# A sequential convolution sweep on TensorE: each tap in four column tiles of 32 outputs instead of two of 64

## The chip, the cores and the metric

One core of one Trainium2 chip runs the whole program. The metric is device time in microseconds (us) of one execution, the median of several. TensorE (PE) multiplies, ScalarE (ACT) and VectorE (DVE) read PSUM and do the elementwise work, GpSimd (POOL) helps a little, and SyncE (SP) issues most DMAs.

## What is computed

The reference is a two-layer network on an image of shape (8, 32, 64, 64): layer norm over channels, a spectral convolution, an expert block on tokens, again a layer norm, then four directional sweeps, and a second expert block. The change touches only the sweeps:

```python
def _sweep(x, w, b, axis, reverse):          # w is (32, 32, 9), b is (32,)
    rows = jnp.moveaxis(x, axis, 0)
    if reverse:
        rows = rows[::-1]
    def step(prev, row):
        new = row + jax.nn.relu(_conv1d(prev, w, b))   # 9 taps along the row, 32 -> 32 channels
        return (new, new)
    _, rest = jax.lax.scan(step, rows[0], rows[1:])
    ...
out = _sweep(x, w_d, b_d, axis=2, reverse=False)
out = _sweep(out, w_u, b_u, axis=2, reverse=True)
out = _sweep(out, w_r, b_r, axis=3, reverse=False)
out = _sweep(out, w_l, b_l, axis=3, reverse=True)
```

Each sweep is a chain of 63 steps, and a step needs the whole result of the step before it. Four sweeps make 252 steps.

## The kernel before

Everything stays in SBUF; all matmuls that matter here are float32. The program is written out by hand for each engine, with semaphores between them, and the order of the text is the order of each engine's queue.

**A step.** A row of 64 positions is folded on the partitions: 4 position groups of 32 channels make 128 partitions, and the 16 positions of a group lie in the free dimension, with one zero column at each end (`state`, four slots). The 9 taps and the folding become three banded 128 x 128 matrices per sweep (`conv_sb[:, s, d]`, d = 0, 1, 2), so that a step is three matmul taps that accumulate in PSUM. The batch of 8 is cut into two halves h of 4 images (64 moving columns each), and each has its own PSUM bank (`conv_bank`), so that one half can be multiplied while the other is being finished.

**Who does what in a step.** PE (lines 673 to 683) waits for a half's state (`s_st`), then issues for each tap d two matmuls, o = 0 and 1, each for 64 of the 128 output rows. The moving operand is the same for both; the weights are a 64-column slice, and the output goes to PSUM partitions 0 to 63 or 64 to 127. This is column tiling: the two matmuls stand in two halves of the array. The last matmul of a half raises `s_cv`. DVE (lines 1085 to 1092) then computes max(conv, -bias) + row + bias in one instruction per half and raises `s_st`, which releases PE for the next step of that half. ACT (lines 809 to 850) adds the bias to the row that comes two steps later (`fetch`, line 811) and copies the new state into the image (`archive`, line 815, `s_arc`).

In the profile every float32 matmul call stands as two weight loads (PEld) and two matmul records (PE): 252 steps x 2 halves x 3 taps x 2 tiles = 3024 calls, 6048 records. The two pairs of a call go to the same column tile and follow each other directly, before the pairs of the next call.

**Loops.** Each sweep does its first three steps straight, then 15 passes of a loop of four steps (`pe.Fori(1, HO)`), on every engine.

**Around the sweeps.** After the second sweep the image is re-folded from rows to columns, after the fourth back again. Both are done by many small DMAs, cut into pieces that are issued while the sweep that writes the data still runs: `move_rows` (line 294; pieces of 5, 5, 4 and 2 groups, 16 DMAs each) and `move_columns` (line 305; three pieces of 16 DMAs, then two half pieces). Each piece waits for `s_arc`. SP issues them; of the last piece POOL issues 6 of 16. On POOL these stand behind `add_conv` (line 317), which adds the finished columns. The third sweep starts when the first columns are there (`wait_columns`, line 288), and the second expert block needs the last columns through `add_conv` on DVE (line 319, called from line 999).

Of the kernel before, what the change touches and what calls it, by code (L numbers as in the profile page):

```python
# [8 lines left out]
B, C, H, W = 8, 32, 64, 64  # L9
# [5 lines left out]
Q = 4  # L15
# [6 lines left out]
HB, MO = B // 2, P // 2  # L22
# [15 lines left out]
def build_kernel(nc, x_in, dft, wspec, conv_w, conv_b, gate_w, gate_b, w1, w2, b2, own, out):  # L38
# [5 lines left out]
    with ExitStack() as ctx:  # L44
        def sb(name, shape, dt=F32):
            return ctx.enter_context(nc.sbuf_tensor(name, shape, dt))
# [14 lines left out]
        conv_sb = sb("conv_sb", [P, 4, 3, P])  # L61
# [61 lines left out]
        def blk(region, n):  # L123

            return region[:, n * P:(n + 1) * P]

        def banks(b0, nb):
            return PS[:, b0:b0 + nb, :].rearrange("p k c -> p (k c)")
# [129 lines left out]
        def half_count(s, t, h):  # L258

            return 2 * row_count(s, t) - 1 + h  # L260

        def state_slot(s, u):

            return (u + 3 * (s % 2)) % 4

        def conv_bank(u, h):

            return PS[:, 2 * h + u % 2, 0:HB * HO].rearrange("p (b v) -> p b v", b=HB)
# [115 lines left out]
        def _(pe):  # L384
# [60 lines left out]
            for l in range(2):  # L445
                m = pe.matmul(PS[:, 6 + l, 0:BL * NE], centre, gate_sb[:, l, :], start=True, stop=True)
# [50 lines left out]
            for c in range(NCH):  # L497
# [5 lines left out]
                for w, full, read in ((1, s_t1, s_tmp), (0, s_t0, s_comb)):  # L503
                    if c >= 2:
                        pe.wait_ge(read, c - 1)
                    for x in range(X8):
                        m = pe.transpose(blk(banks(4 * (c % 2) + 2 * w, 2), x), Z[:, c, x, w], ident)  # L507
# [165 lines left out]
            for s in range(4):  # L673
                def step(q, u):
                    for h in range(2):
                        pe.wait_ge(s_st, half_count(s, Q * q + u - 1, h))
                        for d in range(3):
                            prev = state[:, state_slot(s, u - 1), HB * h:HB * (h + 1), d:d + HO]
                            for o in range(2):
                                m = pe.matmul(conv_bank(u, h)[MO * o:MO * (o + 1)],  # L680
                                              conv_sb[:, s, d, MO * o:MO * (o + 1)], prev,
                                              start=(d == 0), stop=(d == 2))
                        m.then_inc(s_cv, 1)

                for u in range(1, Q):
                    step(0, u)
                with pe.Fori(1, HO) as q:
                    for u in range(Q):
                        step(q, u)
# [480 lines left out]
```

## Time and profile before

| | |
|---|---|
| Median of 3 executions | 669.88 us (669.1 to 671.66) |
| The profiled execution, own time | 670.63 us |
| its span, first to last instruction | 668.8 us |
| mean granted TensorE clock | 0.944 of 2.4 GHz |
| PE / PEld / DVE / ACT / POOL busy | 596.1 / 533.3 / 392.3 / 358.2 / 43.2 us |
| sweeps, from the first matmul to the last DVE result | 308.7 to 564.4 us |
| of that, the re-folding between sweeps 2 and 3 | 431.6 to 442.3 us |

The busy time of PE is that of overlapping records (a record lasts about four times the distance between two), so it says little on how full the array is. The distances between starts and the idle time before an instruction say more. "x24" counts records. The granted clock is 1.00 (2.4 GHz) or 0.50 (1.2 GHz) at any moment; in between are means of a stretch.

### The profile page before, as it was taken

Reading aid. Unit: us, or ns where it says so; the run is one execution under the profiler, and the core shown is the slowest. Engines: PE = TensorE matmul, PEld = TensorE weight load, DVE = VectorE, ACT = ScalarE, POOL = GpSimd, SP = SyncE. Lnnn points to the kernel's source line nnn. Section 1 sums busy time; section 2 is a strip of 40 time slices with the busy share of each in tenths; the row PEclk is TensorE's granted clock in tenths of the full one; section 3 lists DMA queues with packets and bytes.
Section 4 is the critical chain, followed back from the end, with each engine's and each line's share of the span. In section 5 each row is a group of like instructions: output and inputs, shape, how many; then the busy total and the mean of one; then the engine's idle time right before and its main releaser. Section 6 shows DMA issues by size and latency. Waiting matters only on the chain.

```text
span 668.8 us, 23180 instructions
## 1 busy us (share of the span) xinstructions
PE 596.1 (89%) x9536; PEld 533.3 (80%) x9536; DVE 392.3 (59%) x888; ACT 358.2 (54%) x844; POOL 43.2 (6%) x30
## 2 busy tenths in 40 slices
PE   8977886999997999997999999769999999677897
PEld 8877776999996986896888888658888888676883
DVE  3748988555469615554555555425555554498216
ACT  4767987452278101344666666437776665478200
POOL 4000000000030000000000000100000244310000
PEclk9999988999997989996999999969999999897889
DMA  9631771060000000000000032320000334200006
GB/s 360 267 126 30 262 277 68 1 252 1 2 0 1 2 17 0 1 1 1 0 0 0 1 73 61 80 39 0 0 0 2 63 67 79 44 0 1 1 2 251
DMA packets 54386, 40.70 MB, mean 61 GB/s; under 512 B 49350, under 2 KB 49478, under 8 KB 53126
## 3 DMA queue, kind: packets, MB, share of 16 engines
q1 hardware_dynamic: 53816, 39.29, 18.4%
q8 instruction: 33, 0.54, 0.3%
q0 software_dynamic: 384, 0.39, 0.3%
q10 hardware_dynamic: 144, 0.39, 0.2%
q14 instruction: 9, 0.07, 0.0%
HBM read 27.49 MB, written 4.19 MB: 47 GB/s over the span
## 4 chain that ended last, share of the span: by engine, by line
PE 67%; DVE 17%; SPq 6%; ACT 5%; issue 3%; DMA 1%; POOL 0%; ACTq 0%; DVEq 0%
PE PS L680 31%; PE PS L408 6%; DVE RB L940 5%; PE PS L654 5%; PE PS L607 5%; SPq L313 4%; PE PS L429 3%; DVE sums L980 2%; PE PS L483 2%; DVE RCD L992 2%; PE PS L558 2%; PE PS L507 2%; PE PS L514 2%; SPq L302 2%; PE PS L528 2%
## 5 line engine op out<-in xcount | busy, mean ns | idle before, releaser
L680 PE MATMUL PS<-RE,conv_sb 128*64 128x64 f32 x6048 | 238.2, 229 | 18.8 <-DVE RE L1083 8.5
L680 PEld LDWEIGHTS PS<-RE,conv_sb 128*64 128x64 f32 x6048 | 204.8, 140 | 52.5 <-DVE RE L1090 36.6
L1090 DVE SCALAR_TENSOR_TENSOR RE<-PS,negb_sb,RE 128x64 f32<-128x64 f32 x504 | 143.0, 284 | 106.2 <-PE PS L680 80.6
L811 ACT ACTIVATE RE<-RCD,convb_sb 128x128 f32 (+1 forms) x126 | 50.5, 402 | 47.5 <-DVE RE L1090 47.5
L747 ACT COPY RB<-PS 32x128 f32<-32x128 f32 x128 | 47.7, 373 | 8.2 <-PE PS L467 6.8
L940 DVE COPY RB<-PS 32x128 f32<-32x128 f32 x128 | 48.2, 376 | 6.0 <-PE PS L467 4.4
L483 PE MATMUL PS<-RE,RB 128*64 128x64 f32 x1024 | 35.0, 233 | 14.5 <-DVE RCD L949 7.8
L483 PEld LDWEIGHTS PS<-RE,RB 128*64 128x64 f32 x1024 | 33.8, 148 | 16.1 <-DVE RB L940 11.5
L811 ACT ACTIVATE RE<-RE,convb_sb 128x128 f32 (+1 forms) x63 | 32.3, 513 | 20.8 <-DVE RE L1090 15.6
L429 PE MATMUL PS<-warm 128*128 128x128 bf16 x468 | 37.2, 250 | 6.6 <-ACT RCD L787 4.0
L429 PEld LDWEIGHTS PS<-warm 128*128 128x128 bf16 x468 | 34.5, 114 | 7.7 <-ACT RCD L787 4.4
L866 DVE TENSOR_REDUCE sums<-RE 128x32 f32<-128x1024 f32 x16 | 19.4, 1218 | 34.2 <-ACT RE L719 34.2
L811 ACT ACTIVATE RE<-RB,convb_sb 128x128 f32 (+1 forms) x63 | 25.3, 402 | 22.6 <-DVE RE L1090 22.6
L815 ACT COPY RCD<-RE 128x128 f32 (+1 forms) x126 | 35.5, 282 | 1.6 <-DVE RE L1090 1.6
L815 ACT COPY RB<-RE 128x128 f32 (+1 forms) x126 | 35.6, 282 | 1.5 <-DVE RE L1090 1.5
L719 ACT ACTIVATE RE<-PS 128x1024 f32<-128x1024 f32 x16 | 16.2, 1021 | 33.7 <-PE PS L408 33.7
L654 PE MATMUL PS<-RCD,espread 128*128 128x512 f32 x64 | 31.6, 650 | 0.0
L408 PEld LDWEIGHTS PS<-dft_sb,RCD 128*128 128x128 f32 x128 | 30.5, 328 | 0.9 <-issue 0.5
L408 PE MATMUL PS<-dft_sb,RCD 128*128 128x128 f32 x128 | 30.8, 396 | 0.0
L708 ACT COPY RCD<-PS 128x256 f32<-128x256 f32 (+1 forms) x40 | 24.7, 692 | 11.1 <-PE PS L665 6.0
L766 ACT COPY RB<-PS 128x512 f32<-128x512 f32 (+1 forms) x24 | 16.2, 736 | 26.2 <-PE PS L514 26.2
L588 PE MATMUL PS<-proj,RA 128*128 128x192 f32 x128 | 23.8, 348 | 6.1 <-ACT RB L780 5.7
(115 smaller groups left out, 781.2 us busy)
## 6 DMA issues: line engine op xcount, KB each, us to landing
RE<-wspec SPq DMA_DIRECT2D x8, 2048.0 KB, 8.3
RA<-x_in SPq DMA_DIRECT2D x8, 512.0 KB, 7.7
RCD<-x_in SPq DMA_DIRECT2D x1, 4096.0 KB, 13.2
out<-RA SPq DMA_DIRECT2D x8, 512.0 KB, 2.7
RCD<-RB SPq DMA_DIRECT2D x48, 64.0 KB, 2.1
RE<-RCD SPq DMA_DIRECT2D x32, 80.0 KB, 2.2
RE<-RCD SPq DMA_DIRECT2D x16, 64.0 KB, 2.1
RCD<-RB SPq DMA_DIRECT2D x26, 32.0 KB, 1.9
```

The source lines that it names most:

```text
L313: eng.dma_start(CO[C * bl:C * bl + C, k, i, w0:w0 + Q * (v1 - v0)], XF[C * i:C * i + C, Q * v0:Q * v1, BH * bl:BH * bl + BH, :]).then_inc( ...
L408: m = pe.matmul(blk(ln_slot(g), n), src, centre, start=True, stop=True)
L429: pe.matmul(PS[:, bank, 0:P], warm[:, :], warm[:, :], start=True, stop=True)
L483: m = pe.matmul(o[:, x % 2, y], XB[:, c % 2, x, 2 * y + a].rearrange("p r q b -> p (r q b)"), WR[:, c % 3, a, x, y, :], start=True, stop=True)
L607: m = pe.matmul(PS[:, 4 + bh, 0:P], blk(centred(l, 2 * (t // 8) + bh), t % 8), WTOK[:, t, :], start=(t == 0), stop=(t == NT - 1))
L654: pe.matmul(PS[:, 4 + k % 4, :], espread[:, BL * bh:BL * bh + BL, :].rearrange("p b o -> p (b o)"), rhs, start=True, stop=True).then_inc(s ...
L680: m = pe.matmul(conv_bank(u, h)[MO * o:MO * (o + 1)], conv_sb[:, s, d, MO * o:MO * (o + 1)], prev, start=(d == 0), stop=(d == 2))
L747: m = act.copy(o, i)
L811: act.activation(rowb[:, u], row_at(SRC[s], s, q, u), ACT.Identity, bias=convb_sb[:, s:s + 1]).then_inc(s_row, 1)
L815: act.copy(row_at(DST[s], s, q, u), state[:, state_slot(s, u), :, 1:1 + HO]).then_inc(s_arc, 1)
L940: m = dve.tensor_copy(o, i)
L1090: dve.scalar_tensor_tensor(out=state[:, state_slot(s, u), k, 1:1 + HO], in0=conv_bank(u, h), scalar=negb_sb[:, s:s + 1], in1=rowb[:, u, k] ...
```

## The change

One loop of the step is widened: four matmul calls per tap instead of two, each with 32 weight columns and 32 PSUM partitions (`C` is 32, `MO` is 64, `Q` is 4). What is added up is the same, the waits and increments are the same, and the last call of a half still raises `s_cv`.

```diff
                         for d in range(3):
                             prev = state[:, state_slot(s, u - 1), HB * h:HB * (h + 1), d:d + HO]
-                            for o in range(2):
-                                m = pe.matmul(conv_bank(u, h)[MO * o:MO * (o + 1)],
-                                              conv_sb[:, s, d, MO * o:MO * (o + 1)], prev,
+                            for o in range(Q):
+                                m = pe.matmul(conv_bank(u, h)[C * o:C * (o + 1)],
+                                              conv_sb[:, s, d, C * o:C * (o + 1)], prev,
                                               start=(d == 0), stop=(d == 2))
                         m.then_inc(s_cv, 1)
```

PE gets 6048 calls in the sweeps instead of 3024. The other engines' programs do not change.

## Rows read from the trace of the kernel before

**Rows 1.** The page: TensorE in 40 slices, clock, and two groups of its part 5.
```profile
PE   8977886999997999997999999769999999677897
...
PEclk9999988999997989996999999969999999897889
...
L680 PE MATMUL PS<-RE,conv_sb 128*64 128x64 f32 x6048 | 238.2, 229 | 18.8 <-DVE RE L1083 8.5
L680 PEld LDWEIGHTS PS<-RE,conv_sb 128*64 128x64 f32 x6048 | 204.8, 140 | 52.5 <-DVE RE L1090 36.6
L1090 DVE SCALAR_TENSOR_TENSOR RE<-PS,negb_sb,RE 128x64 f32<-128x64 f32 x504 | 143.0, 284 | 106.2 <-PE PS L680 80.6
```
**Rows 2.** Windows, line 680 alone: stretch, its us, busy (records) of PE, of PEld, clock, DMA share, GB/s.
```profile
317.28:431.10 113.82, 109.32 (x2856) 93.04 (x2856) 1.00 0.11 28
...
308.72:314.63 5.91, 5.91 (x106) 5.90 (x108) 0.50 0.00 0
...
442.66:447.75 5.09, 5.08 (x92) 5.08 (x94) 0.50 0.09 14
```
**Rows 3.** Timeline of weight loads and DVE in one step at full clock: start, us, what.
```profile
320.15 0.78 PEld L680 LDWEIGHTS PS<-RE,conv_sb 128*64 128x64 f32 x24 [0.17 <-DVE RE L1090]
...
320.16 0.28 DVE L1090 SCALAR_TENSOR_TENSOR RE<-PS,negb_sb,RE 128x64 f32<-128x64 f32 x1
320.77 0.28 DVE L1090 SCALAR_TENSOR_TENSOR RE<-PS,negb_sb,RE 128x64 f32<-128x64 f32 x1 [0.32 <-PE PS L680]
```
**Rows 4.** Chain of waits and timeline: runs of matmuls elsewhere (start, us, what).
```profile
74.67 3.72 PE PS L483 x120
...
176.44 3.59 PE PS L558 x32
```
**Rows 5.** Windows, line 637 alone (32 weight columns, 8 moving columns).
```profile
245.92:246.33 0.41, 0.41 (x13) 0.41 (x14) 1.00 0.00 0
```
**Rows 6.** Line 680 in windows (full, then half clock) and whole: duration ns least/median/most.
```profile
L680 PEld LDWEIGHTS PS<-RE,conv_sb x4: 133/134/136, 320.1 to 320.2; 128*64 128x64 f32 x4
L680 PE MATMUL PS<-RE,conv_sb x2: 270/270/270, 320.1 to 320.2; 128*64 128x64 f32 x2
...
L680 PE MATMUL PS<-RE,conv_sb x4: 316/342/369, 310.1 to 310.2; 128*64 128x64 f32 x4
...
L680 PE MATMUL PS<-RE,conv_sb x6048: 221/221/369, 308.7 to 563.9; 128*64 128x64 f32 x196
```
**Rows 7.** Windows, line 680, first half step of sweep 3, half clock: records under way.
```profile
442.66:442.70 0.04, 0.03 (x2) 0.03 (x2) 0.50 0.52 74
442.70:442.72 0.02, 0.02 (x2) 0.02 (x2) 0.50 0.26 39
442.72:442.74 0.02, 0.02 (x2) 0.02 (x4) 0.50 0.11 13
442.74:442.82 0.08, 0.08 (x2) 0.08 (x4) 0.50 0.02 2
442.82:442.84 0.02, 0.02 (x4) 0.02 (x5) 0.50 0.00 0
442.84:442.90 0.06, 0.06 (x4) 0.06 (x6) 0.50 0.00 0
442.90:442.94 0.04, 0.04 (x5) 0.04 (x4) 0.50 0.00 0
```
**Rows 8.** Timeline of DVE: the step after the first loop pass, and both ends.
```profile
316.87 0.70 DVE L1090 SCALAR_TENSOR_TENSOR RE<-PS,negb_sb,RE 128x64 f32<-128x64 f32 x2 [0.26 <-PE PS L680]
317.90 0.63 DVE L1090 SCALAR_TENSOR_TENSOR RE<-PS,negb_sb,RE 128x64 f32<-128x64 f32 x2 [0.33 <-PE PS L680]
...
430.98 0.63 DVE L1090 SCALAR_TENSOR_TENSOR RE<-PS,negb_sb,RE 128x64 f32<-128x64 f32 x2 [0.32 <-PE PS L680]
...
563.78 0.64 DVE L1090 SCALAR_TENSOR_TENSOR RE<-PS,negb_sb,RE 128x64 f32<-128x64 f32 x2 [0.32 <-PE PS L680]
...
578.94 1.92 DVE L319 TENSOR_TENSOR RA<-RCD 128x1024 f32<-128x1024 f32 x1 [8.80 <-DMA RCD<-RB]
```
**Rows 9.** Timeline of the issuing queues, SP and POOL, at both re-foldings.
```profile
424.71 10.42 SPq L302 DMA_DIRECT2D RE<-RCD  x16
...
432.25 3.62 POOL L302 DMA_DIRECT2D RE<-RCD  x6 [230.61 <-ACT RCD L815]
...
560.58 16.98 SPq L313 DMA_DIRECT2D RCD<-RB  x26
...
562.06 5.69 POOL L319 TENSOR_TENSOR RA<-RCD 128x1024 f32<-128x1024 f32 x2 [9.51 <-DMA RCD<-RB]
```
**Rows 10.** The page, part 3: the queue that carries TensorE's instructions.
```profile
q8 instruction: 33, 0.54, 0.3%
```

## The prediction

> **What bounds the kernel now.** I read the page first. TensorE is busy in nearly every slice, and the costliest groups are the sweeps' matmuls and weight loads and the DVE instruction that answers them [rows 1]. Busy says little here, since a record lasts four to eight times the distance to the next. So I read the windows: at full clock 2856 records, that is 119 steps of 24, take 113.82 us, or 0.956 us a step [rows 2]. Then one step in the timeline: the 24 weight loads cover 0.78 us, and before them PEld was idle for 0.17 us and waited for DVE [rows 3]. So the step is a latency chain and not yet a full array. For one half it is: PE's 12 records, the drain, 0.28 us of DVE, the way back.
>
> The change alters only PE's part, so I need to know when a matmul really starts.
>
> *How long an array slot is.* Line 558 streams 128 columns with 128-column weights: 32 records in 3.59 us, 0.112 each, so 0.056 for 64 columns [rows 4]. Line 483 has the shape and the two tiles of line 680: 120 records in 3.72 us, less the 0.22 of the last record [rows 6], are 0.0294 each, two in 0.0588 [rows 4]. So two column tiles each do one record in about the time one record needs alone: they do overlap. I call 0.0585 us a slot, with 0.056 as the lower bound. Before, a half is six slots.
>
> *What starts when.* The first half step of sweep 3 comes after a long pause, at half clock, with both tiles empty [rows 7]. At 442.66 to .70 the first call's two loads and two matmuls are on record (two each). By 442.74 the second call's loads have begun too (four loads). But up to 442.82 there are still only two matmuls; the third starts at about 442.83. How long does a 64-column load take? The first matmuls show it: 270 ns where the normal one is 221 at full clock, and 369 where it is 316 at half clock (most and least of the window of four) [rows 6], so some 0.05 us at either clock. The second tile's weights, started by 442.74, are there by 442.79, and its part of the array is empty. Its matmul still waits until about 442.83. That is just when the first call's first record has streamed (from 442.72, for the 0.107 us of a slot at half clock) and its second record can begin. My reading: matmuls start in program order, across tiles. A record that waits for its own tile holds up those behind it, whichever tile they are for.
>
> **The change, part by part.**
>
> *1. Matmuls.* With this rule, number the records of a tap: T0a T0b T1a T1b T2a T2b T3a T3b. Each b is for the same tile as its a and starts one slot later. T1a starts with T0b, T1b a slot later with T2a, and so on: every slot starts two records, as before. Two tiles overlap, never four. A tap has 8 records, so four slots; a half has 12 slots instead of 6, a step 24. At 0.0585 that is 1.404 us.
>
> Is that the bound, or still the chain? The chain of a half was 0.956 us, and gets six slots longer (0.351) and a shorter first load. Loads of 32 columns come 13 to 14 in 0.41 us [rows 5], 0.031 each instead of the 0.05 above, so 0.02 off. The chain is then 1.29 us, below 1.404. So PE's idle 0.17 us goes, PE becomes the bound, and DVE and ACT get slack. The extra 1 to 2 hundredths of shorter loading are hidden in a full array.
>
> Sweeps 1 and 2 run from 308.72 to 431.61 (430.98 + 0.63), 122.9 us [rows 2, 8]. After: the first 5.9 us are at half clock [rows 2], where a slot is 0.107 and a step 2.57, so 2.3 steps; the other 123.7 take 173.7; drain and the last DVE 0.5. Sum 180.1, +57.2. Sweeps 3 and 4, 442.66 to 564.42: 121.8 us. After: 5.1 at half clock (2.0 steps), 124.0 x 1.404 = 174.1, 0.5: 179.7, +57.9. I assume the clock comes back after as long a time; TensorE is at least as busy as before. Together **+115.1 us**. With 0.056 as the slot it would be 15 less, with 0.0588 2 more.
>
> *2. The loop's branch.* The step after the first pass comes 1.03 us after its predecessor instead of 0.956 [rows 8]: going back costs 0.07 more than the 0.17 us of idle time hides. In later passes it is hidden. That cover is now gone. Each of the 60 passes may cost from nothing (if enough instructions are queued ahead) to 0.24 us, 0 to 14 in all. Twice the instructions also means that a queue of a given depth covers less. I take 0.08, **+5 us**; the sum of the sweeps is so much larger that I do not refine it.
>
> *3. DMA pieces.* SP needs 10.42 us for 16 issues [rows 9]. The last two pieces of `move_rows` are 8 steps apart, 7.65 us now. So SP, which began at 424.71, is free only at 435.1, while POOL, with the same wait, began at 432.25. With 8 steps of 1.40 = 11.2 us SP is free in time: **-3 us**, as the columns' landing starts sweep 3. At the other end SP issues 26 DMAs from 560.58 without a pause to 577.56 [rows 9], though the last state was there at 564.4: it was late already at 560.58. After, only the last 10 issues (6.5 us) and 1.9 for landing follow the last step: 9 instead of 14.5 us until DVE's line 319 at 578.94 [rows 8]. POOL's adds also end before the last step instead of at 567.75. DVE had been idle for 8.80 us before line 319; POOL's and ACT's squares of the next stage start to show, so of 5.5 I take **-4.5**. Bounds together -9 to 0.
>
> Nothing else moves: ACT, DVE and POOL have the same instructions. The sum is 115.1 + 5 - 7.5 = +112.6 us. On the profiled execution's 670.63 that is 783.2; the median lies 0.75 below, so **782.5 us**. The bounds above (-15 to +2, -5 to +9, -1.5 to +7.5) add up to 761 to 801; they will hardly all fall to one side, so 764 to 798.
>
> **The rivals.**
>
> *Four tiles at once (faster).* If each tile had its own queue, T1a, T2a, T3a would start a few hundredths apart, a half would stay at six slots, the first load would be 0.02 to 0.027 shorter, and the last tile would start about 0.02 after the first instead of 0.0585. The chain would lose 0.06 us: 252 x 0.06 = 15, so 655 us. For it: two tiles do overlap fully [rows 4]. Against it: the empty second tile that waits in [rows 7]. It decides whether T1a starts before T0b. The Trainium skill has this as its rule: "TensorEngine Tiling (Array Packing)", When to Use Tiling, gives four column tiles for 32 columns, and "TensorE: Matmul & The Clock Gate", Part 3, has matmuls in different tiles start about 4 ns apart. The same Part 3 says that matmuls start and end strictly in order, which [rows 7] agree with; its bursts have one matmul per tile and not a pair that must follow each other. Chance 0.08.
>
> *Only the loads are in order (a little slower).* If matmuls were free but weight loads dispatched in order, the next tile would be held by one load of 0.031 per record pair. A tap is then 4 x 0.031 = 0.126 instead of 0.117, the end of a half 0.03 later, 252 x 0.03 = +8: 678 us. The second tile's matmul in [rows 7] waits 0.04 longer than its load would explain. Chance 0.05.
>
> *Worse than two at a time.* Either 32-column tiles do not overlap at all (48 slots, 2.8 us a step, about 1125 us), or the longer loop body does not stay in TensorE's instruction store. The body of four steps grows from about 196 to 388 instructions (four times 24 or 48 pairs of load and matmul, and a few of the loop). Queue 8 moved 0.54 MB in 33 packets in the whole program [rows 10], so the 60 passes now run without a refetch, but no row shows how much fits. A fetch of a microsecond or two in 30 to 60 passes would be 50 to 100 us on top, 830 to 880. The Trainium skill, "Runtime: NRT & Kernel Launch", Instruction fetch mechanics, speaks both of a store on TensorE that would hold the body and of a window of two pages that a branch must stay in; no run here has shown either. Chance 0.05.
>
> *No effect.* The widened loop is unconditional and lies on every step, so only an exact cancelling would give it: 0.02.
>
> **How the numbers follow.** Forecast 0.80, with its own range 764 to 798. That range leaves out the others, 0.20, so it is the range given. What this kernel's measurement can tell from no change is about 0.5%, 3.4 us. Faster by more: 0.08. Within: 0.02. Slower: 0.80 + 0.05 + 0.05 = 0.90.
>
> **What would show it.** In the profile after: 12096 records of line 680 in each of PE and PEld; at full clock a step of 1.39 to 1.42 us; no or little idle time of PE inside the sweeps; DVE's wait per half longer. In windows of the first half step of sweep 3, the matmuls still start two per slot, at 0.107. The PE side of line 1090's waits grows. SP begins the last piece of `move_rows` within a microsecond of POOL. If instead the step is near 0.90 us, matmuls do not wait across tiles, and my reading of [rows 7] is wrong; if it is 0.98, loads pace them. If steps are 1.40 but four-step passes are far above 5.7, the branch or the fetch costs more than I took. If PE shows a slot other than 0.0585 for 32 columns, the size of the term is off, not its sign.

## The result, and the profile after

| | before | after |
|---|---|---|
| median of 20 executions each, us | 670.16 (667.05 to 672.52) | 674.71 (670.94 to 678.59) |
| ratio | | 1.0069, 95% interval 1.0049 to 1.0089 |
| profiled execution, own time / span, us | 670.63 / 668.8 | 673.60 / 671.8 |
| mean granted clock | 0.944 | 0.947 |
| step at full clock, us | 0.956 | 0.950 |

The kernel became slower by 4.6 us, 0.7%. The forecast was +112.6 us. The sign was right by luck, for a reason that turned out to be false. The profiled executions differ by 3.0 us; only these can be taken apart below, and what the medians differ by beyond that no trace shows.

The page after, in the parts that answer to [rows 1] and [rows 10]:

```profile
span 671.8 us, 35276 instructions
...
PE   8977877999997999988999899669999999577897
...
PEclk9999989999997989996999999959999999897889
...
q8 instruction: 38, 0.62, 0.4%
...
L680 PE MATMUL PS<-RE,conv_sb 128*32 128x64 f32 x12096 | 228.8, 225 | 30.3 <-DVE RE L1083 8.5
...
L680 PEld LDWEIGHTS PS<-RE,conv_sb 128*32 128x32 f32 x12096 | 188.6, 111 | 70.8 <-DVE RE L1090 58.4
...
L1090 DVE SCALAR_TENSOR_TENSOR RE<-PS,negb_sb,RE 128x64 f32<-128x64 f32 x504 | 142.8, 284 | 108.4 <-PE PS L680 86.2
```

The number of records has doubled, 6048 to 12096, and yet PE is busy for less time and sits idle *more*: before the weight loads 70.8 us instead of 52.5, and still waiting for DVE. PE has not become the bound. The instruction queue moved 38 packets instead of 33.

Windows of line 680 after (stretch, its us, busy and records of PE, of PEld, clock, DMA share, GB/s), and one step in the timeline, which answer to [rows 2, 3]:

```profile
392.00:430.00 38.00, 35.67 (x1920) 29.43 (x1920) 1.00 0.31 78
```
```profile
330.08 0.72 PEld L680 LDWEIGHTS PS<-RE,conv_sb 128*32 128x32 f32 x48 [0.23 <-DVE RE L1090]
...
330.08 0.28 DVE L1090 SCALAR_TENSOR_TENSOR RE<-PS,negb_sb,RE 128x64 f32<-128x64 f32 x1
330.69 0.28 DVE L1090 SCALAR_TENSOR_TENSOR RE<-PS,negb_sb,RE 128x64 f32<-128x64 f32 x1 [0.33 <-PE PS L680]
```

1920 records are 40 steps of 48, in 38.00 us: 0.950 us a step. 48 loads now take 0.72 us where 24 took 0.78, and the idle time grew from 0.17 to 0.23. The latency chain is what it was.

**Four matmuls at once.** The same stretch as [rows 7], at half clock. (That stretch is called the first half step of sweep 3; it belongs to the second step. The first step, 24 records, had run at 438.09 before, and runs at 438.94 after.)

```profile
441.81:441.85 0.04, 0.03 (x4) 0.03 (x5) 0.50 0.48 68
...
441.89:441.96 0.07, 0.07 (x8) 0.07 (x12) 0.50 0.03 4
...
441.98:442.04 0.06, 0.06 (x9) 0.06 (x9) 0.50 0.00 0
```

Four matmul records are under way where two were, and eight about a slot later. [Rows 7] had two, then four. Each slot has simply doubled its content. With the forecast's rule (T0b holds back T1b and all behind it) this could not be.

**Where the 3.0 us of the profiled executions went.** Line 680's first record comes 0.44 us earlier and DVE's last result 1.64 us later, so the sweeps with the re-folding take 2.1 us longer. The steady steps gave back 252 x 0.0065 = 1.6. Against that stand four things, each read as the lengthening of DVE's steps against the steady one.

*First, TensorE stopped for code.* Weight loads in the first pass of sweep 2's loop, in the timeline:

```profile
373.06 0.26 PEld L680 LDWEIGHTS PS<-RE,conv_sb 128*32 128x32 f32 x15 [0.30 <-DVE RE L1090]
373.93 0.12 PEld L680 LDWEIGHTS PS<-RE,conv_sb 128*32 128x32 f32 x4 [0.61 <-issue]
...
375.99 0.33 PEld L680 LDWEIGHTS PS<-RE,conv_sb 128*32 128x32 f32 x15
377.37 0.14 PEld L680 LDWEIGHTS PS<-RE,conv_sb 128*32 128x32 f32 x2 [1.05 <-issue]
```

"issue" says that the engine waited for nothing that the profile shows. The middle of a half, after 15 loads, has no semaphore to wait for. From load to load the two stops are 0.72 and 1.16 us instead of about 0.01 to 0.05; a third of 0.42 us stands at 510.16, in sweep 4's first pass. The first two lie exactly 256 TensorE instructions apart. Together the three are 2.3 us, and they lengthen the steps by 1.9, since some idle time would have been there anyway. In the whole trace before there is no such stop inside the sweeps. The fetch packets on the instruction queue start about 1.2 us after TensorE enters each such block of 256, and the block behind can be used 2.2 us after that here, and up to 2.75 us in the runs below: 3.4 to 4.0 us for a block of new code. Two tiles use up 256 instructions in 5.1 us, four in 2.5 to 2.7. These stops stand in first passes of a loop, where the code is new.

*Second, the slow clock lasted longer.* TensorE has little or nothing to do between sweeps 2 and 3. Windows before, then after (all engines; the clock is the third number from the end):

```profile
434.00:438.00 4.00, 0.00 (x0) 0.00 (x0) 0.18 (x2) 0.18 (x1) 1.87 (x4) 0.51 0.61 118
...
447.00:452.00 5.00, 5.00 (x123) 4.45 (x121) 2.88 (x11) 3.40 (x10) 0.00 (x0) 0.92 0.01 3
```
```profile
434.00:438.00 4.00, 0.00 (x0) 0.00 (x0) 0.00 (x0) 0.00 (x0) 2.68 (x5) 0.87 0.69 140
...
447.00:452.00 5.00, 4.79 (x194) 4.46 (x190) 2.27 (x8) 2.42 (x8) 0.00 (x0) 0.64 0.02 3
```

The clock fell at 434.1 before and at 437.0 after, in the middle of a pause that ended nearly alike, and it came back at 447.8 and at 450.6. Much of the difference passed in waiting for the columns' DMAs: from sweep 3's first record to DVE's third step it is 6.98 us before and 7.02 after. Of the four steps behind that, two ran at half clock before and all or most of four after (1.28 us and not 0.95); they take 4.50 us before and 4.99 after. So the slow clock cost about 0.5 us.

*Third*, the step that follows the first pass of a loop is 1.23 us instead of 0.96 in sweep 2 and 1.39 instead of 1.03 in sweep 3; in sweeps 1 and 4 the two kernels are within 0.02 of each other. Together that is 0.7 us.

*Fourth*, the later passes are not free. Their first steps are now and then longer, most of all in sweep 3's fifth pass, beside one more fetch packet at 463.43:

```profile
462.80 0.62 DVE L1090 SCALAR_TENSOR_TENSOR RE<-PS,negb_sb,RE 128x64 f32<-128x64 f32 x2 [0.33 <-PE PS L680]
463.90 0.62 DVE L1090 SCALAR_TENSOR_TENSOR RE<-PS,negb_sb,RE 128x64 f32<-128x64 f32 x2 [0.47 <-PE PS L680]
```

That step is 1.09 us; the others are up to 1.05. All later passes together cost 0.5 us more than in the trace before. -1.6 + 1.9 + 0.5 + 0.7 + 0.5 is 2.0, against the measured 2.1.

The rest, 1.4 us, is lost behind the sweeps, between DVE's last result and its line 319 (14.52 us before, 15.92 after). The end in the timeline, as in [rows 8, 9]:

```profile
559.56 21.03 SPq L313 DMA_DIRECT2D RCD<-RB  x30
...
565.41 0.64 DVE L1090 SCALAR_TENSOR_TENSOR RE<-PS,negb_sb,RE 128x64 f32<-128x64 f32 x2 [0.31 <-PE PS L680]
...
581.97 1.92 DVE L319 TENSOR_TENSOR RA<-RCD 128x1024 f32<-128x1024 f32 x1 [10.19 <-DMA RCD<-RB]
```

SP's issues cost 0.65 us each before (16.98 for 26), 30 of them 19.6; here they took 21.03, since a single one, at 574.07, took 1.95. DVE's line 319 begins 3.03 us later than in [rows 8], and the span is 3.0 us longer.

The long issue is bound up with TensorE's code too. A fetch packet on TensorE's instruction queue runs from 574.16 to 575.60. In the 13 traces of this document 15 issues of the re-foldings are longer than 1 us (1.08 to 1.95), and every one overlaps such a packet. Of the re-foldings' DMAs 37 took over 2.6 us from issue to landing (the median is 2.07), and 36 of them were under way during one. The trace before has its long issue as well, 1.63 us at 439.51 beside a packet at 439.36, but in the first re-folding. Where a packet falls into the last issues, the pause before line 319 is 15.6 to 16.3 us in the kernels with a step of 0.90 to 0.96 us; in the two without one there (before and e7) it is 14.5. The one trace of before has no packet in this stretch; the changed kernel, e9, which is the same kernel again, and e11, which has its four tiles in reverse, all have one. What is shown is the coincidence, in every trace; no run moves the fetch alone. (Packet times are those of the traces' DMA records.)

### The profile page after: what moved, and what is told of

Same layout as the page of the kernel before. It is cut to its first block, busy times and chain, and to the rows that moved or that the text cites. A ratio compares the mean times of both kernels' runs of the same rounds, so it can differ in the third digit from the quotient of the medians.

```text
span 671.8 us, 35276 instructions
## 1 busy us (share of the span) xinstructions
PE 585.3 (87%) x15584; PEld 515.7 (77%) x15584; DVE 392.2 (58%) x888; ACT 358.4 (53%) x844; POOL 43.4 (6%) x30
## 4 chain that ended last, share of the span: by engine, by line
PE 57%; DVE 25%; SPq 6%; ACT 5%; issue 5%; DMA 1%; POOL 0%; ACTq 0%; DVEq 0%
PE PS L680 21%; DVE RE L1090 9%; PE PS L408 6%; DVE RB L940 5%; PE PS L654 5%; PE PS L607 5%; SPq L313 4%; PE PS L429 3%; DVE sums L980 2%; SPq L302 2%; DVE RCD L992 2%; PE PS L558 2%; PE PS L483 2%; PE PS L507 2%; PE PS L514 2%
## 5 line engine op out<-in xcount | busy, mean ns | idle before, releaser
L680 PE MATMUL PS<-RE,conv_sb 128*32 128x64 f32 x12096 | 228.8, 225 | 30.3 <-DVE RE L1083 8.5
L680 PEld LDWEIGHTS PS<-RE,conv_sb 128*32 128x32 f32 x12096 | 188.6, 111 | 70.8 <-DVE RE L1090 58.4
L483 PE MATMUL PS<-RE,RB 128*64 128x64 f32 x1024 | 34.1, 230 | 15.6 <-DVE RCD L949 8.1
```

What stands on the lines that cost most here:

```text
L483: m = pe.matmul(o[:, x % 2, y], XB[:, c % 2, x, 2 * y + a].rearrange("p r q b -> p (r q b)"), WR[:, c % 3, a, x, y, :], start=True, stop=True)
L680: m = pe.matmul(conv_bank(u, h)[C * o:C * (o + 1)], conv_sb[:, s, d, C * o:C * (o + 1)], prev, start=(d == 0), stop=(d == 2))
```

## The experiments

The question after the result was not whether four tiles overlap, but which rule gives 0.950 us, and why the kernel is nevertheless slower. I took four groups of runs: the order of the calls, the number and the width of tiles, where the code stands, and no tiles at all. Totals of single runs scatter by some 0.4%, so in the first two groups I compare the step at full clock, read from the distances of DVE's records.

### Order of the calls

**e1_tile_major_64.** Two tiles of 64, but all taps of tile 0 before those of tile 1.

```diff
-for d in range(3):
-    for o in range(2):
+for o in range(2):
+    for d in range(3):
```

> Two tiles of 64 as before, but the three taps of tile 0 are issued first and then the three of tile 1 (o outside, d inside). Theory A (each tile takes its records as they come, calls to another tile pass a call that waits, as far as TensorE looks ahead): if it looks ahead six records or more, the step stays at 0.956 us at full clock; if only to the next call, the tiles run one after the other, some 11 to 12 slots of 0.0585 a half, 1.29 to 1.40 us a step. Theory B (the strict order of the prediction, with two records a slot only because neighbouring calls are for different tiles): 11 slots a half, 1.3 to 1.4 us a step, total 755 to 785 us.

Measured: 705.1 us (before beside it: 673.38), and a step of 1.113 us, between the two expectations. Windows of line 680 in one half, which was released at 340.155:

```profile
340.16:340.26 0.10, 0.10 (x1) 0.10 (x2) 1.00 0.00 0
...
340.31:340.32 0.01, 0.01 (x2) 0.01 (x2) 1.00 0.00 0
340.32:340.33 0.01, 0.01 (x4) 0.01 (x4) 1.00 0.00 0
...
340.38:340.43 0.05, 0.05 (x5) 0.05 (x5) 1.00 0.00 0
...
340.49:340.54 0.05, 0.05 (x7) 0.05 (x6) 1.00 0.00 0
340.55:340.60 0.05, 0.05 (x8) 0.05 (x6) 1.00 0.00 0
```

A record stays under way for 0.22 us and a tile starts one every 0.0585, so one tile alone can have four under way. There are five at 340.38 and eight at 340.55 (one of these is the next half's first): the second tile's records have started while the first tile's were not through. By their starts, tile 0 begins at 2, 109, 168, 225, 281 and 340 ns after the release; tile 1 at 174, 284, 343, 399, 457 and 515. **The record at 174 stands in the program behind those at 225, 281 and 340.** It lasts 271 ns, as a tile's first record does (in e3 the first of a half lasts 222 to 271, most often 270, and the others 220 to 222). So matmuls do not start in program order across tiles. Within a tile they do. But there is a limit: tile 1's first load comes at 172, when the third of tile 0's six records has begun. TensorE looks past a few waiting records of a tile, not past five.

**e2_tile_major_32.** The same swap of the two loops with four tiles of 32.

> Four tiles of 32, tile by tile (o outside, d inside). Theory A with wide look-ahead: 0.95 us a step as in the changed kernel. Theory A with look-ahead of one call, or B: four tiles of six records nearly one after the other, about 21 to 24 slots a half, 2.4 to 2.8 us a step, total above 1000 us. A value in between tells how many calls TensorE looks ahead.

Measured: 757.64 us, step 1.327. The first loads of the four tiles come at 0, 142, 285 and 427 ns: each tile starts 2.5 slots behind the one before. The same limited look-ahead, three times over. Order matters a great deal (0.950 against 1.327 us) although it never forces one tile to wait for another's whole work.

These two kernels give one thing more. Their steps are long, as my forecast had it of the change, and so they test its step 3. The pause before sweep 3 and the one before line 319 in e1, and the same two in e2 (timeline of DVE). Before they were 6.20 us, as the first line shows, and 8.80 [rows 8].

```profile
437.82 0.34 DVE L1083 COPY RE<-RE 128x64 f32<-128x64 f32 x2 [6.20 <-DMA RE<-RCD]
```

```profile
457.12 0.34 DVE L1083 COPY RE<-RE 128x64 f32<-128x64 f32 x2 [5.22 <-DMA RE<-RCD]
...
615.03 1.97 DVE L319 TENSOR_TENSOR RA<-RCD 128x1024 f32<-128x1024 f32 x1 [6.34 <-DMA RCD<-RB]
```
```profile
483.86 0.34 DVE L1083 COPY RE<-RE 128x64 f32<-128x64 f32 x2 [4.24 <-DMA RE<-RCD]
...
664.37 1.97 DVE L319 TENSOR_TENSOR RA<-RCD 128x1024 f32<-128x1024 f32 x1 [3.86 <-DMA RCD<-RB]
```

In e2 the pauses are 1.96 and 4.94 us shorter, 6.9 together. 252 x (1.327 - 0.956) = 93.5, less 6.9, is 86.6; its profiled time is 87.0 above before's. In e1 the same sum is 39.6 - 3.4 = 36.1 against a measured 34.5.

### Number and width of the tiles

Each of these leaves out part of the outputs, as its expectation says, and is read for its step alone.

```diff
-for o in range(Q):
+for o in range(1):   # e8: one tile of 32; e4: range(2), e7: range(3); e3: one tile of 64, from range(2) of before
```

> Only o = 0 of the two tiles of 64: the outputs of the upper 64 partitions are left out, so the result is not the reference's. Shows which records stand 0.007 us apart. If the pairs of before are two tiles, the six records of a half now stand alone, 0.056 to 0.058 apart, and the step is 0.95 us (the 0.007 between tiles saved). If the pairs are the two records of one call, pairs remain, and a slot for a pair of one tile would be 0.117: the same distance between calls as before, 0.117, with nothing in between. Total 666 to 670 us either way.

> Two tiles of 32 (o = 0, 1): the outputs of partitions 64 to 127 are left out, so the result is not the reference's. Same number of instructions as before, the short weight loads of the change. Theory: against before the first load is 0.025 us shorter and nothing else changes, so the step is 0.93 us at full clock, 252 steps x 0.025 = 6 us less than before, 664 us. The changed kernel's 0.95 then means that two more tiles cost 0.02 us a step. If it is 0.95 too, the shorter load gives only 0.006 whatever the number of tiles. No waits for code in the first pass of the loops, since the code is as long as before.

> Three tiles of 32; the outputs of partitions 96 to 127 are left out, so the result is not the reference's. One tile of 64 gave 0.939 us a step and two 0.956; two of 32 gave 0.917 and four 0.950: 0.017 for each further tile at either width. If that is the price of a tile, this is 0.933 to 0.935. If only the step from two to four costs (a limit of two at a time for something), it is 0.917 or 0.950.

> One tile of 32; the outputs of partitions 32 to 127 are left out, so the result is not the reference's. So far 0.917 (two tiles of 32), 0.934 (three), 0.950 (four): 0.0165 a tile. If the price is per tile from the first on and the width costs 0.039 (0.956 against 0.917 with two tiles), one tile of 32 gives 0.900, and the two terms are independent (one tile of 64 gave 0.939). If the width matters only beside a second tile, it is 0.92 or more.

| tiles x width | step, us | last record of a half starts, ns | from there to DVE, ns |
|---|---|---|---|
| 1 x 64 (e3) | 0.939 | 343 | 259 |
| 2 x 64 (before) | 0.956 | 349 | 270 |
| 1 x 32 (e8) | 0.900 | 306 | 257 |
| 2 x 32 (e4) | 0.917 | 313 | 266 |
| 3 x 32 (e7) | 0.934 | 318 | 277 |
| 4 x 32 (after) | 0.950 | 326 | 288 |

The starts are counted from the weight load that DVE releases. e3 came out at 0.939 us where 0.95 was expected and e4 at 0.917 where 0.93 was, the first for the 11 ns between the last record and DVE, the second for slightly shorter slots; e7 and e8 came out as expected. Timeline of DVE in e3, then in e8:

```profile
395.37 0.65 DVE L1090 SCALAR_TENSOR_TENSOR RE<-PS,negb_sb,RE 128x64 f32<-128x64 f32 x2 [0.29 <-PE PS L680]
396.31 0.28 DVE L1090 SCALAR_TENSOR_TENSOR RE<-PS,negb_sb,RE 128x64 f32<-128x64 f32 x1 [0.29 <-PE PS L680]
```
```profile
340.56 0.62 DVE L1090 SCALAR_TENSOR_TENSOR RE<-PS,negb_sb,RE 128x64 f32<-128x64 f32 x2 [0.28 <-PE PS L680]
341.46 0.62 DVE L1090 SCALAR_TENSOR_TENSOR RE<-PS,negb_sb,RE 128x64 f32<-128x64 f32 x2 [0.28 <-PE PS L680]
```

From 395.37 to 396.31 is e3's step, 0.94 us, from 340.56 to 341.46 e8's, 0.90. The table reads as two prices. **Halving the width at equal number gives 0.039 us a step** (e3 to e8, before to e4). 25 ns of it is one load: in before the second record starts 107 ns behind the first, with 32 columns 82. Some 10 ns are the four slots from the second record to the sixth, 0.056 instead of 0.0584 each, and 2 to 4 ns lie before DVE. **Each further tile costs 0.0165 us a step** (three times with 32 columns, once with 64): its records start 6.5 ns behind the tile before, and then about 11 ns more pass between the last record and DVE. The change halves the width and adds two tiles: -0.039 + 0.033 = -0.006.

These are steps inside a pass. e7 loses 4.1 us at the ends of its later passes, up to 0.31 at one of them, where the change loses 0.6 in all. No run explains that.

e3 also shows how [rows 7] should have been read. With one tile, single records stand where before has pairs 7 ns apart (2, 109, 167, ... against 2 and 9, 109 and 116, ...). A pair is two tiles' records of the same rank, and not the two records of a call.

**e11_tiles_reversed.** Tiles in the order 3, 2, 1, 0, to see whether the 11 ns belong to the place of the last tile or to the number of tiles.

```diff
-for o in range(Q):
+for o in reversed(range(Q)):
```

> The changed kernel with its four tiles issued in the order 3, 2, 1, 0. Half of a tile's price of 0.017 us is that its last matmul is issued 0.0065 later; the rest, 0.011 a tile, lies between the last matmul's start and DVE's (0.259 us with one tile of 64, 0.270 with two; 0.266, 0.277, 0.288 with two, three and four of 32). If that rest belongs to the number of matmuls that stream at once, the step stays at 0.950 and the 0.288 too. If it belongs to a place (tiles further up being later), the reverse order gives 0.91 to 0.93.

Windows, all engines:

```profile
392.00:430.00 38.00, 35.39 (x1924) 29.04 (x1920) 22.56 (x81) 23.35 (x80) 0.00 (x0) 1.00 0.30 75
```

Measured: 674.3 us in one run, 40 steps in 38.00 us as after, and 287 ns from the last record to DVE. The price goes with the number of tiles. Why TensorE needs it stays open.

### Where the code stands

**e5_loop_only** has four tiles in the loop bodies and two in the three straight steps, **e6_straight_only** the reverse. Both compute everything. Together with them ran **e9_change_again**, the change itself.

```diff
-def step(q, u):
+def step(q, u, n):
+    w = P // n
...
-    step(0, u)
+    step(0, u, 2)        # e6: 4
...
-        step(q, u)
+        step(q, u, 4)    # e6: 2
```

> The change in the loops only (60 of the 252 step slots in the code, 240 of the steps run); the three straight steps of each sweep keep two tiles of 64. Two theories of why the changed kernel gains nothing although its step is 0.0065 us shorter. Theory C (code): instructions that run for the first time come in pages of 256, and a page cannot be there sooner than some 3.4 us after the one before it, while four tiles use up a page in 2.5 us. Then the page borders of this kernel fall, by counting its instructions, at instruction 321 of the first pass of sweep 2, 296 of sweep 3 and 271 of sweep 4 with a full page before them in new code; waits of 0.5 to 1 us stand there, in the middle of a step at a weight load that waits for no semaphore, and none at the first page border of a loop. Sum 2 to 3 us against a gain of 240 x 0.0065 = 1.6: 0.5 to 1.5 us slower than before. Theory D (no code waits matter, the loss lies in the moved DMA pieces): no such waits, 1.6 us faster.

> The change in the three straight steps of each sweep only; the loops keep two tiles of 64. Theory C: the full-page distances in new code lie at instruction -31 (third straight step) of sweep 2 and 15 of the loop of sweep 4; some 0.5 to 0.8 us each, nothing in sweeps 1 and 3, which begin at half clock. 12 steps x 0.0065 are nothing: +1.0 to 1.5 us against before. Theory D: no change within 0.3 us.

> The changed kernel itself, on the same chip as the two halves of the change, so that the three compare: +3 to +6 us against before (0.7%), more than the sum of the two halves if page borders and the clock after sweep 3's start add up.

| | ratio to before (95%) | steady step | code stops, us | sweeps 1+2 and 3+4, us |
|---|---|---|---|---|
| before | | 0.956 | none | 248.7 |
| e5 | 1.0023 (0.9998 to 1.0047) | 0.950 | 0.54, 0.32, 0.68, 0.92 | 248.9 |
| e6 | 0.9995 (0.9968 to 1.0022) | 0.956 | 0.9, 0.3 | 249.2 |
| e9 | 1.0064 (1.0039 to 1.0089) | 0.950 | 0.89, 1.70, 0.43 | 250.8 |
| after | 1.0069 (1.0049 to 1.0089) | 0.950 | 0.72, 1.16, 0.42 | 250.7 |

(Last column: first record of line 680 to DVE's last start in sweep 2, plus the same for sweeps 3 and 4. Stops are from load to load, so 0.1 above the idle time in the rows.) Three of e5's stops in the timeline, then e6's. Beside the four of the table e5 has two small ones, 0.18 and 0.21, in later passes of sweep 4.

```profile
376.77 0.13 PEld L681 LDWEIGHTS PS<-RE,conv_sb 128*32 128x32 f32 x4 [0.21 <-issue]
...
447.47 0.14 PEld L681 LDWEIGHTS PS<-RE,conv_sb 128*32 128x32 f32 x5 [0.57 <-issue]
...
508.12 0.15 PEld L681 LDWEIGHTS PS<-RE,conv_sb 128*32 128x32 f32 x8 [0.82 <-issue]
```
```profile
372.96 0.14 PEld L681 LDWEIGHTS PS<-RE,conv_sb 128*32 128x32 f32 x6 [0.81 <-issue]
...
506.24 0.19 PEld L681 LDWEIGHTS PS<-RE,conv_sb 128*64 128x64 f32 x3 [0.20 <-issue]
```

The stops moved to the places that followed from counting blocks of 256 instructions in each program: three of e5's four, and both of e6's. e5's first, 0.54 us in sweep 1, had not been expected. e6's second one even stands in front of a load of the old width: what waits is not four tiles as such but the block that comes too soon behind another. They are stops for code.

In time the expectations did not come true as clearly. e6 was to be 1.0 to 1.5 us slower, and the interval of each of the two takes in no change. In the sweeps the halves of the change cost 0.2 and 0.5 us against 2.0 for the whole, and that is not because e5 had fewer stops: its four are 2.5 us, its later passes cost another 0.9, and 240 steps x 0.0065 give back only 1.6. The balance comes from the beginning of sweep 3. From its first record to DVE's third step e5 takes 5.89 us, against 6.98 before, 7.02 after, 6.75 in e6 and 6.80 in e9. In each of these four a fetch packet fell among the last DMAs of the columns, and in e5 none did. The kernels with fewer tiles agree: 5.75 to 5.84 us in e3, e7 and e8, without a packet there, and 7.06 in e4, with one. So the two halves do not add up to the whole, and a part of each difference is where the fetches happen to fall. e9 repeats the change's excess, stops and long step included.

The Trainium skill, "Runtime: NRT & Kernel Launch", Instruction fetch mechanics, has TensorE's code come in blocks of 256 instructions, each fetched while the one before is executed, at a cost that is "mostly hidden". The blocks agree with the distances here. "Mostly hidden" holds for two tiles in this kernel and not for four, with stops of 0.3 to 1.7 us.

### No column tiles

**e10_one_call_128.** One call a tap for all 128 outputs, to see what the tiling itself is worth.

```diff
-for o in range(Q):
-    m = pe.matmul(conv_bank(u, h)[C * o:C * (o + 1)],
-                  conv_sb[:, s, d, C * o:C * (o + 1)], prev,
+m = pe.matmul(conv_bank(u, h), conv_sb[:, s, d, :], prev,
```

> One call per tap with all 128 outputs, no column tiles; computes the same. By the theory that a half waits for one weight load and then six slots, each slot the longer of load and stream: the load of 128 columns is 0.107, the stream still 0.053, so slots of 0.112 bound by the load: the last matmul of a half starts about 0.107 + 5 x 0.112 = 0.67 us after the release instead of 0.35, and PE is full: 12 x 0.112 = 1.34 us a step against a chain of 1.26 to 1.28. Step 1.34 us, total about 765 us. If loads of an untiled matmul were faster than that, the step would be near 0.94.

```profile
span 1060.2 us, 17132 instructions
...
PEclk9999999998975555555555555555555555558898
```
```profile
392.00:430.00 38.00, 38.00 (x180) 38.00 (x180) 8.52 (x30) 8.84 (x30) 0.00 (x0) 0.50 0.00 0
```

Measured: 1061.97 us, far above the expected. DVE's steps are 2.56 us apart, 0.213 us a record, and the granted clock was 0.50 all through the sweeps although PE had a record under way all the time. The clock went otherwise than I had supposed; it can account for at most a factor of two, and 2.56 against the expected 1.34 is 1.9. There are two readings of the slot. If a load of 128 columns takes twice as long at half clock, 0.213 us is that load alone, as the expectation had it. If it does not, load and stream took turns. The starts of the records speak for the second: a matmul starts 0.101 us after its load, and the next load 0.112 us after the matmul, which is about the 0.107 that a stream of 64 columns lasts at 0.50 (the slot of [rows 7]). No run decides it. Why the clock stayed down, and whether a full 128-column load always shuts out the stream, this run does not tell; line 558 [rows 4] has 128 weight columns with 128 moving ones and keeps 0.112 a record. The run says that, at the clock that each kernel was given, the first split, into two tiles, was the large one.

## Why the prediction was right or wrong

**What bounds the kernel: right.** A latency chain, not a full array. It stayed so after the change, with more idle time of PE than before.

**The slot: right, and it decided nothing.** 0.0585 us for 64 columns, 0.056 with 32-column tiles, both named as bounds.

***What starts when*: this is the step that failed.** [Rows 7] show two records, later four. I took the first two for the two records of one call and built on that "matmuls start in program order, across tiles". They were the first records of two tiles. What I took for an empty second tile that waits was a second tile already at work, and what waited was each tile's own second record. The prediction held the contradicting fact itself: the second record of a call starts a slot behind its first, so two records *at once* cannot be one call's. e1 shows the overtaking directly, e3 the single records, the trace after four at once.

**Step 1, +115.1 us: false, worth -1.6.** A half keeps six slots; each holds four records. (The sum also took sweep 3 to start at 442.66, where its second step starts, and so counted one step of 1.4 us too many.) One term inside it was right: the shorter first load, put at 0.02 us, measured 25 ns.

**Step 2, the loop's branch, +5 us: false in size and place.** PE did not become the bound, and the idle time still hides most of the branch: the later passes cost 0.5 us together. That it can cost more shows in e7, with 4.1 us. What I had named among the rivals as a matter of the loop *body* appeared as a matter of *new* code: 2.3 us of stops in first passes, and a step of 1.23 and 1.39 us behind the first passes of sweeps 2 and 3. And there was no term for what comes with a fetch among SP's issues, 1.4 us at the end.

**Step 3, -7.5 us: right as a rule, empty here.** With a step of 1.33 us the two pauses shrink by 6.9 us (e2). With 0.950 they do not: at the first re-folding SP takes 17.34 us for 26 issues, long past POOL's start at 433.06, as in [rows 9].

```profile
425.57 17.34 SPq L302 DMA_DIRECT2D RE<-RCD  x26
...
433.06 3.62 POOL L302 DMA_DIRECT2D RE<-RCD  x6 [231.68 <-ACT RCD L815]
```

**The rivals.** "Four tiles at once" was the mechanism, at a chance of 0.08, but its price was off: 0.06 us a step less, where 0.006 was measured. It counted two gains. The load was about right: 25 ns, and some 10 from four shorter slots. The other was not there: it let the last tile's start move from 0.0585 to 0.02 us behind the first, which is again the false reading of the kernel before; in truth it moved from 7 to 20 ns, a loss of 13. And it did not know the 11 ns that each further tile adds before DVE, nor the stops for code. So the outcome, this mechanism and slightly slower, was no case of mine.

The Trainium skill had both sides. "TensorEngine Tiling (Array Packing)", When to Use Tiling, says that 32 columns allow four tiles; the trace after agrees. "TensorE: Matmul & The Clock Gate", Part 3, says that matmuls start and end strictly in order, which I let speak for my reading; where tiles differ, e1's record at 174 ns goes against it.

**The range** was built round one reading of seven rows, with a chance of 0.80 on it, and that reading moves the time by 17%. The rows could have contradicted it. By the strict rule the first slot of a half holds a single record, T0a, and the last a single one too, seven starts in all; [rows 7] have a pair from the first moment, and at full clock before's last pair starts at 343 and 349 ns, in the sixth place and not a slot later.

## What to carry to other kernels

Before inferring an order from overlapping records, settle which record belongs to which operand, best with a run that has only one of them. Column tiles take up their records independently of each other, as far as TensorE looks ahead: while the moving columns per tile stayed the same, more tiles of smaller width made this chain shorter only by the smaller load and slightly shorter slots, and every tile added to the latency. Interleave tiles tap by tap, since TensorE looks only a few records past a busy tile. And where instructions are doubled, look at the first pass over each loop body, for there the code itself can come too late, and look at which DMAs are being issued when a block is fetched.

## What the runs showed of the hardware that I had not expected

- Matmuls of different column tiles overtake each other, with a look-ahead of a few records: calls tile by tile start each tile 0.142 us (four tiles) or 0.172 us (two) behind the last.
- A further column tile costs 0.0165 us per step of two halves: 6.5 ns of start and about 11 ns between last record and reader. The latter has no explanation here.
- New TensorE code came at 3.4 to 4.0 us per 256 instructions; four-tile code consumed them in 2.5 to 2.7 us and stopped for 0.3 to 1.7 us at a time.
- Without column tiles the clock stayed at 1.2 GHz through sweeps in which PE had records under way all the time, and a record took 0.213 us.
- SP's DMA issues that overlapped a fetch of TensorE's code took up to 1.95 us instead of 0.65, and DMAs under way then landed in up to 3.66 us instead of 2.07.
- Between sweeps 2 and 3 the slow clock lasted 13.65 us both before and after and only fell 2.86 us later, so that it also ended 2.86 us later. In e5 it lasted 10.2 us and in e2 6.8.
